# A gated linear-attention layer on eight cores: the bf16 state copy is written before the f32 one, and one transpose evacuation moves from DVE to ACT

## The reference

```
xn = layernorm(x)
q, k = swish(xn @ Wq), swish(xn @ Wk);  v = xn @ Wv
f = log_sigmoid(xn @ Wf) / 8;  s = 1 - exp(f)
per token t, per head:
    hk = hk * exp(f_t) + k_t (outer) s_t          # 256 x 64 state
    p  = softmax((q_t / 16) @ hk)
    hv = hv * exp(f_t) + s_t (outer) v_t          # 64 x 256 state
    o_t = p @ hv
attn = (o * rsqrt(mean(o*o) + 1e-5) * g_norm_w) @ Wo
xp = xn shifted by one token
ffn = sigmoid(mix(xn, xp, mu_r) @ W_r) * (relu(mix(xn, xp, mu_k) @ W_k)**2 @ W_v)
out = x + attn + ffn
```

## Time and profile before

| | |
|---|---|
| median of 3 timed runs | 1912.95 us |
| profiled execution | 1909.7 us |
| span of its slowest core (core 5) | 1908.2 us |
| spans of the eight cores | 1902.1 to 1908.2 us |
| PE busy in the span | 1293.7 us (68%) |
| DVE busy | 803.1 us (42%) |
| ACT busy | 495.7 us (26%) |
| POOL busy | 81.7 us (4%) |
| mean granted TensorE clock, core 5 | 0.756 |
| chain that ended last | PE 53%, DVE 23%, ACT 9%, issue 7%, DMA 5% |

### The profile page before, as it was taken

How to read it: one execution, slowest core, us unless ns; L and a number is a source line. 1 busy time by engine, 2 the same in 40 slices (tenths; PEclk the granted TensorE clock), 3 DMA queues, 4 the chain that set the end, 5 groups by cost and what they waited for, 6 DMA issues and landing times.

```text
span 1908.2 us, 23006 instructions; the slowest of 8 cores (1902.1 to 1908.2 us)
## 1 busy us (share of the span) xinstructions
PE 1293.7 (68%) x8172; PEld 781.9 (41%) x8172; DVE 803.1 (42%) x1857; ACT 495.7 (26%) x1073; POOL 81.7 (4%) x112
## 2 busy tenths in 40 slices
PE   2407595866859586675958668595866759586774
PEld 1203262534426253442625344262534426253442
DVE  2234434354343435434343543434354343435433
ACT  1102232222223232222323222232322223232221
POOL 1000000000000000000000000000000000000000
PEclk9756596877859587785958778596867859586786
DMA  5870000000000000000000000000000000000000
GB/s 171 257 239 23 11 12 33 12 23 22 23 12 12 34 12 22 23 23 12 12 33 12 23 23 23 12 12 33 12 23 23 23 12 12 34 12 23 23 1 23
DMA packets 19136, 65.77 MB, mean 34 GB/s; under 512 B 2256, under 2 KB 3664, under 8 KB 19024
## 3 DMA queue, kind: packets, MB, share of 16 engines
q0 software_dynamic: 12736, 47.19, 7.0%
q1 hardware_dynamic: 6288, 17.12, 2.8%
HBM read 47.52 MB, written 16.78 MB: 34 GB/s over the span
## 4 chain that ended last, share of the span: by engine, by line
PE 53%; DVE 23%; ACT 9%; issue 7%; DMA 5%; DVEq 1%; SPq 0%; ACTq 0%; POOL 0%; POOLq 0%
PE pB L167 18%; PE pA L167 15%; PE pC L167 8%; PE pF L167 5%; PE pD L167 3%; DVE hv L828 3%; PE pE L167 3%; PE pT L172 2%; DVE lnscr L296 2%; DVE tmp L780 1%; DVE hv_bf L833 1%; DVE fstage L583 1%; DVE tmp L578 1%; DVE hk_sb L784 1%; ACT L500 1%
## 5 line engine op out<-in xcount | busy, mean ns | idle before, releaser
L167 PE MATMUL pC<-wo_sb,xn_bf 128*128 128x512 bf16 x256 | 111.0, 613 | 48.1 <-DVE xn_bf L887 33.3
L661 ACT ACTIVATE t_l<-t_e,t_linv 128x256 f32<-128x256 f32 x32 | 16.2, 507 | 374.5 <-DVE t_linv L644 374.5
L167 PE MATMUL pA<-wrt_sb,fstage 128*128 128x512 bf16 x256 | 62.5, 388 | 63.8 <-DVE xtail L468 63.8
L172 PE MATMUL pT<-identb_sb,xn_bf 128*128 128x128 bf16 x256 | 32.4, 306 | 90.4 <-DVE xnT L359 49.5
L492 DVE TENSOR_TENSOR Am_sb<-pD,mask_sb 128x512 bf16<-128x512 f32 x16 | 11.1, 692 | 178.9 <-PE pD L167 178.8
L167 PE MATMUL pD<-v_sb,spp 128*64 128x256 bf16 x64 | 19.6, 410 | 96.7 <-ACT o_bf L800 96.7
L172 PE MATMUL pT<-identb_sb,k_sb 128*128 128x128 bf16 x256 | 33.2, 273 | 75.9 <-ACT kT_sb L675 75.9
L507 DVE CAST l_hi<-t_l 128x512 bf16<-128x512 f32 x16 | 6.8, 427 | 183.2 <-ACT t_l L503 183.2
L913 DVE TENSOR_TENSOR ob<-pC,fstage 128x512 f32<-128x512 f32 x32 | 22.1, 692 | 133.2 <-PE pC L167 133.2
L167 PE MATMUL pA<-wvt_sb,xnT 128*128 128x512 bf16 x256 | 61.1, 382 | 24.4 <-DVE xnT L534 17.5
L167 PEld LDWEIGHTS pC<-wo_sb,xn_bf 128*128 128x128 bf16 x256 | 32.9, 138 | 109.0 <-issue 109.0
(11 more groups left out here) (163 smaller groups left out, 2676.4 us busy)
## 6 DMA issues: line engine op xcount, KB each, us to landing
out<-ob POOLq DMA_DIRECT2D x32, 512.0 KB, 2.9
xb<-x POOLq DMA_DIRECT2D x30, 512.0 KB, 5.2
stage<-wq POOLq DMA_DIRECT2D x2, 1024.0 KB, 8.5
fstage<-wq SPq DMA_DIRECT2D x2, 1024.0 KB, 8.7
fstage<-wk SPq DMA_DIRECT2D x2, 1024.0 KB, 6.3
stage<-wk POOLq DMA_DIRECT2D x2, 1024.0 KB, 5.9
fstage<-wv SPq DMA_DIRECT2D x2, 1024.0 KB, 6.2
stage<-wv POOLq DMA_DIRECT2D x2, 1024.0 KB, 7.1
```

Of the source, the lines that this page charges most:

```text
L167: e.matmul(out=o, lhsT=l, rhs=r, start=st, stop=sp),
L172: lambda e, o=out_ap, i=in_ap, d=ident: e.transpose(out=o, in_=i, identity=d),
```

## The change

There are two edits. In `emit_R_hb` the sum of `hk_tmp` and pF is first written as bf16 into `hk_bf`, after which the count `hkbf_done` is taken, and then computed a second time into the f32 `hk_sb`; before, it was computed once into `hk_sb` and cast. In the very first chunk both are copies of pF in the same order. In `emit_R_tail_b` both halves of `oT_sb` are copied by ACT, and the first `wo` matmul waits for ACT's count alone.

```diff
--- before.py
+++ after.py
@@ -773,20 +773,24 @@
                        inc="T" if (h == 3 and ii == 1) else None)
             hk_done = val("T")
             if first:
+                em("vector", lambda e: e.tensor_copy(out=hk_bf[:], in_=pF[:, 0:512]),
+                   waits=[("T", hk_done), ("V", val("V"))], inc="V")
+                hkbf_done[0] = val("V")
                 em("vector", lambda e: e.tensor_copy(out=hk_sb[:], in_=pF[:, 0:512]),
-                   waits=[("T", hk_done), ("V", val("V"))])
+                   waits=[("V", val("V"))], inc="V")
             else:
                 for ii in range(2):
                     em("vector", lambda e, ii=ii: e.tensor_tensor(
                         out=hk_tmp[:, ii * 256:(ii + 1) * 256],
                         in0=hk_sb[:, ii * 256:(ii + 1) * 256], in1=lbc_sb[:], op=ALU.mult),
                        waits=[("T", hk_done), ("V", val("V"))] if ii == 0 else ())
+                em("vector", lambda e: e.tensor_tensor(out=hk_bf[:], in0=hk_tmp[:],
+                                                       in1=pF[:, 0:512], op=ALU.add),
+                   waits=[("V", val("V"))], inc="V")
+                hkbf_done[0] = val("V")
                 em("vector", lambda e: e.tensor_tensor(out=hk_sb[:], in0=hk_tmp[:],
                                                        in1=pF[:, 0:512], op=ALU.add),
-                   waits=[("V", val("V"))])
-            em("vector", lambda e: e.tensor_copy(out=hk_bf[:], in_=hk_sb[:]),
-               waits=[("V", val("V"))], inc="V")
-            hkbf_done[0] = val("V")
+                   waits=[("V", val("V"))], inc="V")
             reader(pF, "V")
 
             return st
@@ -883,26 +887,18 @@
                     tr(bank[:, ii * 128:(ii + 1) * 128], o_bf[:, i * 128:(i + 1) * 128],
                        identb[:], waits=w, inc="T" if ii == 3 else None)
                 tdone = val("T")
-                if r == 0:
-                    em("vector", lambda e, r=r, b=bank, j=j: e.tensor_copy(
-                        out=oT_sb[:, j * 1024 + r * 512: j * 1024 + (r + 1) * 512],
-                        in_=b[:, 0:512]),
-                       waits=[("T", tdone), ("V", val("V"))], inc="V")
-                    reader(bank, "V")
-                    oTv = val("V")
-                else:
-                    em("scalar", lambda e, r=r, b=bank, j=j: e.copy(
-                        out=oT_sb[:, j * 1024 + r * 512: j * 1024 + (r + 1) * 512],
-                        in_=b[:, 0:512]),
-                       waits=[("T", tdone)], inc="S")
-                    reader(bank, "S")
+                em("scalar", lambda e, r=r, b=bank, j=j: e.copy(
+                    out=oT_sb[:, j * 1024 + r * 512: j * 1024 + (r + 1) * 512],
+                    in_=b[:, 0:512]),
+                   waits=[("T", tdone)], inc="S")
+                reader(bank, "S")
             oT_done = val("S")
             obf_free[0] = val("T")
 
             for h2 in range(2):
                 bank = (pC, pF)[h2]
                 for i in range(8):
-                    w = ([("S", oT_done), ("V", oTv)] + bank_gates(bank)) if i == 0 else ()
+                    w = ([("S", oT_done)] + bank_gates(bank)) if i == 0 else ()
                     mm(bank[:, 0:512], oT_sb[:, j * 1024 + i * 128: j * 1024 + (i + 1) * 128],
                        w_sb["wo"][:, i * 1024 + h2 * 512: i * 1024 + h2 * 512 + 512],
                        start=(i == 0), stop=(i == 7), waits=w, inc="T" if i == 7 else None)
```

## The result

The changed kernel's median is 1884.1 us against 1912.8 us, and the ratio is 0.985 (95% interval 0.984 to 0.987), which is 28 us less. In some executions of either kernel the cores of one die run at a lower granted clock and take longer; the medians include them, the ratios do not. The forecast was 1885.4 us.

What follows compares the result with a forecast made beforehand. No engine is full; PE stands at hand-overs. Gains of 8.5 + 17.4 - 1.3 = 24.6 us plus 3 for the clock make 27.6, taking the median from 1912.95 to 1885.4 us; 8-in-10 range 1879 to 1898.

Steps and rivals of the forecast that it cites:

- The bf16 state first: Chunk 0's state update: `hk_bf` ready 0.53 us earlier, second sum hidden behind the logits matmuls; 8.5 us over sixteen.
- the cover: Chunk 0's second sum on DVE ends 0.28 us before the softmax L636 of chunk 1 is wanted, so it stays hidden.
- Both copies on ACT, chunk 0: Output projection of chunk 0 no longer waits for DVE's copy and starts 1.09 us earlier; 17.4 us over sixteen.
- Both copies on ACT, chunk 1: Output projection of chunk 1, where the engines had copied side by side: a loss of 0.08 us, 1.3 us over sixteen.
- this sign of being right: Chunk 1's projection would start 0.1 us later behind its transposes.
- The clock: Half-clock stretches behind the projections: all superchunks of the shorter kind, about 109.1 us without alternation; 3 us gained.
- A: Half-clock stretches behind both projections become long, taking back up to 17.6 us; time 1906, half of it 1897; chance 13%.
- B: Second sum on DVE in chunk 0 is not hidden, so `hk_bf`'s gain goes; 1896.9 without the clock's term; chance 12%.
- C: Slower: the clock rises only after all 16 matmuls of chunk 0's projection, net 10 us lost, time 1923; chance 3%.
- D: No change: PE's three waits are only exchanged for others that end as late; chance 4%.
- S: Experiments' theory: the path's parts and the clock's part add up, so each edit is worth its own time.
- P: Experiments' theory: clock rises do not move with the kernel; superchunk lengths settle, so edits gain nothing, their time, or more.

Runs made afterwards that it cites:

- third sum: Changed kernel with the second, f32 sum of the state update made twice: 1887.0 us, ratio 0.985 (0.979 to 0.992).
- late cast: Changed kernel with chunk 1's bf16 cast of the value state moved on DVE behind the copies of the next xn: 1879.6 us, ratio 0.983.
- first edit alone: Kernel before with only the bf16 state summed ahead of the f32 state, output copies still by DVE and ACT: 1909.8 us, ratio 0.9997.
- early chain: Late cast kernel with chunk 1's RMS chain also moved between the two halves of the value state's update: 1870.6 us, ratio 0.978.
- first edit undone: Half casts kernel with the state again summed in f32 and then cast: 1855.0 us, ratio 0.968.
- half casts: Early chain kernel with chunk 0's value-state cast split in two, the first half ahead of the update's second half: 1836.0 us, ratio 0.960.
- second edit alone: Kernel before with only both output copies on ACT, state update as before: 1888.7 us, ratio 0.989.
- 0.53 us added: Changed kernel with one more small DVE instruction in each of the 32 state updates: 1888.7 us, ratio 0.989.

## Why the prediction was right

- **The bf16 state first.** Forecast 0.53 us in each chunk 0, hidden second sum with 0.28 us to spare; measured 0.53 and 0.28. The third sum showed that the cover ends where it was said to.
- **Both copies on ACT, chunk 0.** Forecast 1.09, measured 1.20 (9.47 to 8.27 from chunk 1's output to the projection). PE starts 0.15 after the second copy's end, not 0.25.
- **Both copies on ACT, chunk 1.** Forecast a loss of 0.08, measured a gain of 0.04, for the same reason; this sign of being right did not come. The three terms together are 1.77 us or 28.3 us in all where 24.6 were forecast.
- **The clock.** Forecast: all superchunks of the kind with a long stretch in chunk 0 (4.5) and a short one in chunk 1 (2.9), no alternation, 109.1 us, and 3 us more than the path. Measured: this pattern, on all eight cores, with 4.7 and 3.2 us and a length of 109.21. The two stretches together went from 8.2 to 7.9 us, and half of that is 0.13 us per superchunk or 2 us in all.
- **Rivals.** A (stretches long and long) was not seen in the changed kernel. It was one small saving away: with the late cast the stretches are 5.5 and 4.4 us and take back all that was saved. B was refuted by the row of L636, which PE still releases; the second sum does cost the 0.69 us that the prediction took for it. C and D did not occur. In C's sum 4.85 should read 4.8, which changes nothing.

So the mechanism was right and the total is in part luck of small errors: the path was 3.7 us better than forecast and the clock's term 1 us worse, and the first superchunks and the last gained less than the 1.89 us of those between.

One thing in the working was not right, though the total did not show it: the clock was treated as a term beside the others. With that the first edit was said to be worth 8.5 us, and alone it is worth nothing measurable. Alone it also costs 0.26 us ahead of DVE's copy, which only the second edit takes away. The length is always the path and half of the half-clock stretches, but the stretches depend on where the path puts the projections against the rises, so no edit has a worth of its own: the edit was worth 0, 5 to 7 and 18 us in three surroundings, and 0.8 us off the path of the changed kernel left its superchunks where they were.

Neither theory came out whole. S fails on the first edit alone, on the late cast, on the early chain and on the first edit undone among the half casts. P in its strict form fails on the second edit alone and on the 0.53 us added, where S is within the error. What holds is P's premise, that the rises come at distances of their own, and the sum of path and half clock. Averaged over the whole table the length does follow the path (4.2 us of path from the kernel before to the half casts, 4.7 us of length), but in steps. The change happened to end on the edge of a step from which the path's sum is nearly exact, and that was luck. Not settled is what fixes the distances between the rises, and with them the height of the steps.

## What to carry to other kernels

Where PE falls to half clock in each iteration, an edit's worth must be measured together with its neighbours: a result of "no change" can mean that the saving was swallowed by the stretch behind it, and the next small saving may then bring both. Look in the trace at the lengths of single iterations, not only at the total: equal lengths to 0.02 us after an edit that did shorten a wait are the sign. And look on an in-order queue for work that nobody waits for standing ahead of work that is waited for; edits of that kind, with the split cast, brought 104 us here (1884 to 1780), against the 28 of the change. Where a start looks late on single cores only, count the matmul records of that group first.

## What was not expected of the hardware

- The superchunk lengths of two different kernels (before and first edit alone) agree within 0.02 us from the fourth superchunk on, an outlier of 112.62 us included. Six cores of each kernel have this sequence within 0.03 us; the other two have 110.93 us on average instead of 111.10, at the same program and path.
- The rises of the granted clock behind the projection of chunk 1 are 102.40, 105.81, 109.23 or 112.64 us apart from one superchunk to the next, in twelve kernels and on eight cores, and nothing between.
- With a path 0.8 us shorter the length stayed at 109.20 against 109.21 us; with 1.5 us shorter single superchunks fell to 106.6.
- PE started 0.15 us after the end of the second of two ACT copies; in the kernel before, with one copy, 0.25 us.
